# Four graph layers on one core: node steps between layer 2 and layer 3 run per half of the nodes

## The reference

```python
h = relu(layernorm(x)); x = x + relu((adj @ h) @ W.T + b)            # layer 0
h = relu(layernorm(x)); h, q, k = three Lorentz linear maps           # layer 1
att = adj * sigmoid((2 + 2 * (qm @ k.T)) / att_scale + att_bias)
support = att @ h; x = x + support / sqrt(|inner(support)|)
h = relu(layernorm(x))                                                # layer 2
w = adj / deg; log_ij = logmap(h_i, h_j)                              # for every pair i, j
agg = einsum('ij,ijc->ic', w, log_ij); x = x + expmap(0, agg @ weight + bias)
h = relu(layernorm(x)); x = x + w_last100(adj) @ (h @ weight) + bias  # layer 3
```

## Time and profile before

| | before |
|---|---|
| median of 3 runs | 1219.32 us (1218.47 to 1220.24) |
| profiled execution: time, span | 1219.28 us, 1217.5 us |
| PE, DVE, ACT, POOL busy | 89%, 70%, 62%, 32% of the span |
| mean granted TensorE clock | 0.94 |

### The profile page before, as it was taken

One profiled execution on the slowest core, in us unless ns is written; L12 is line 12 of the kernel. 1 busy time (PEld: TensorE's weight loads), 2 busy tenths in 40 slices (PEclk: granted clock), 3 DMA queues, 4 the chain that ended last, 5 costly groups with the idle time before them and its releaser, 6 DMA issues.

```text
span 1217.5 us, 15886 instructions
## 1 busy us (share of the span) xinstructions
PE 1081.6 (89%) x5064; PEld 503.5 (41%) x5084; DVE 851.6 (70%) x916; ACT 760.8 (62%) x780; POOL 393.4 (32%) x279
## 2 busy tenths in 40 slices
PE   2799999997699999999159999999999999954997
PEld 0233333336523333333124554555545454443555
DVE  7799989976756666666836767667677777666553
ACT  2355555552556666665258778778787888635864
POOL 6434423420101111110163334333343434323533
PEclk9799999997789999999569999999999999966999
DMA  9799999960068888885304545535454545211652
GB/s 325 263 351 358 350 341 339 359 250 9 1 196 287 280 281 286 288 281 180 128 0 140 171 133 179 173 124 187 139 173 138 181 131 157 67 54 44 205 184 86
DMA packets 96286, 237.97 MB, mean 195 GB/s; under 512 B 16369, under 2 KB 45041, under 8 KB 79857
## 3 DMA queue, kind: packets, MB, share of 16 engines
q1 hardware_dynamic: 87024, 220.62, 54.7%
q10 hardware_dynamic: 9216, 16.78, 3.6%
HBM read 219.55 MB, written 17.83 MB: 195 GB/s over the span
## 4 chain that ended last, share of the span: by engine, by line
PE 82%; DVE 8%; POOL 3%; issue 3%; ACT 2%; DMA 1%; SPq 0%; DVEq 0%; POOLq 0%; ACTq 0%
PE PS L452 55%; PE PS L649 10%; PE PS L595 5%; PE PS L596 4%; PE PS L672 4%; PE PS L484 1%; PE PS L462 1%; PE PS L474 1%; DVE st L1024 1%; DVE work L1021 1%; PE PS L696 1%; POOL work L408 1%; ACT work L766 1%; POOL X L401 1%; POOL brow L375 1%
## 5 line engine op out<-in xcount | busy, mean ns | idle before, releaser
L1161 DVE TENSOR_TENSOR work<-work,ring 128x1024 f32<-128x1024 f32 x128 | 151.2, 1222 | 88.6 <-ACT work L858 88.6
L415 POOL TENSOR_TENSOR ring<-work,ring 128x1024 f32<-128x1024 f32 x58 | 137.2, 2365 | 214.5 <-DVE work L1248 214.5
L801 ACT ACTIVATE work<-PS 128x1024 uint8<-128x1024 f32 x128 | 124.1, 1021 | 130.4 <-PE PS L452 130.4
L858 ACT ACTIVATE work<-PS,att_sc 128x1024 f32<-128x1024 f32 x128 | 147.4, 1201 | 88.7 <-PE PS L596 45.3
L452 PE MATMUL PS<-work,ystage 128*64 128x512 f32 x768 | 186.3, 606 | 0.1
L452 PE MATMUL PS<-ring,work 128*65 128x256 f32 (+1 forms) x568 | 183.2, 469 | 2.6 <-DVE work L1275 2.6
L1242 DVE SCALAR_TENSOR_TENSOR work<-PS,work 128x1024 f32<-128x1024 f32 x72 | 88.2, 1225 | 120.8 <-PE PS L452 107.6
L649 PE MATMUL PS<-TB,TA 65*128 65x512 f32 x288 | 139.8, 609 | 4.7 <-DVE work L1242 2.9
L381 POOL COPY ystage<-H 128x64 f32 x60 | 83.2, 1387 | 137.2 <-PE PS L452 136.9
L452 PEld LDWEIGHTS PS<-ring,work 128*65 128x65 f32 x568 | 77.2, 138 | 84.7 <-issue 62.8
L897 ACT ACTIVATE work<-work 128x1024 f32<-128x1024 f32 x72 | 76.0, 1055 | 46.1 <-DVE work L1242 45.9
(11 more groups left out here) (203 smaller groups left out, 1637.8 us busy)
## 6 DMA issues: line engine op xcount, KB each, us to landing
ring<-in_adj_t SPq DMA_DIRECT2D x96, 1024.0 KB, 5.2
ring<-in_adj_t SPq DMA_DIRECT2D x100, 512.0 KB, 3.8
work<-in_adj_t SPq DMA_DIRECT2D x32, 1024.0 KB, 7.7
...
```

The source lines that it names most:

```text
L415: nc.gpsimd.tensor_tensor(near(n), sum_[:, n % ROTS, :], near(n), ALU.mult).then_inc(sem("near_ready"), 1)
L801: nc.scalar.activation(made[:, k, u * UNIT:(u + 1) * UNIT], PS[:, (4 + 2 * u) * BANK:(6 + 2 * u) * BANK], ACT.Relu).then_inc(sem("codes_ma ...
L858: nc.scalar.activation(att[:, u % 2, :], PS[:, b * BANK:(b + 2) * BANK], ACT.Sigmoid, bias=att_sc[:, 2:3], scale=att_sc[:, 1:2]).then_inc( ...
L1161: V.tensor_tensor(prob[:, u, :], att[:, u % 2, :], ring[:, s, (u % 2) * UNIT:(u % 2 + 1) * UNIT], ALU.mult)\
```

## The change

- **Start.** The layernorm of layer 0 runs for group 1 alone first; that of group 0 stands between the first masks and degrees. POOL has four `ystage` buffers (`STAGES`) and starts at the first group; each of the eight bias pieces stands behind one staged tile.
- **Layer 1** is written out without loops, first all 32 source tiles for the first half of the targets, then for the second (64 steps). Weights are read from `HL` directly; POOL stages nothing.
- **First half's node steps** stand behind single steps of the second half's gather (`first_half1(o)`, o = 0 to 31).
- **Second half's node steps** stand behind units 0 to 13 (`second_half2(n)`); its rows are flipped behind units 12 and 13 (`FLIP1`).
- **Units** are in another order: 20 within the first half, 32 mixed (all mirrored), 20 within the second half; 12 segments where there were 8 strips.
- The `sums`, `Zn`, `GA` and `kap` buffers lie at other places, and loads for the first units start as ring slots come free.

```diff
-UNITS = [(S, p) for S in range(NS) for p in range(2 * S, T // 2)]
+UNITS = ([(S, p) for S in range(NS // 2) for p in range(2 * S, T // 4)]
+         + [(S, p) for S in range(NS // 2) for p in range(T // 4, T // 2)]
+         + [(S, p) for S in range(NS // 2, NS) for p in range(2 * S, T // 2)])
 NU = len(UNITS)
+N0 = sum(p < T // 4 for S, p in UNITS)
+FLIP1 = 12
...
+            for s in range(TG):
+                if s >= STAGES:
+                    pool.wait_ge(sem("agg0_done"), s - STAGES + 1)
+                nc.gpsimd.tensor_copy(ystage[:, s % STAGES, 0:D], H[:, T - 1 - s, :]).then_inc(sem("staged0"), 1)
+                if s >= STAGES:
+                    bias_piece(s - STAGES)
+            pool.wait_ge(sem("feats0_ready"), G)
...
+            def first_half1(o):
+                if o == 3:
+                    pe.wait_ge(sem("sums_out1"), 1)
+                    to_nodes(ident[:, :], 0, 0).then_inc(sem("support_ready"), 1)
+                if o == 18:
+                    pe.wait_ge(sem("support_used"), 1)
+                    pe.wait_ge(sem("zn_ready"), 1)
+                    flip_rows(PS[0:ROWS, 0:UNIT], 0, TG // 2).then_inc(sem("z_flipped"), 1)
+                if o == 22:
+                    pe.wait_ge(sem("zr_out"), 1)
+                    pe.wait_ge(sem("zl_out"), 1)
+                    pe.wait_ge(sem("kap_l_ready"), 1)
+                    flip_rows(PS[0:ROWS, 0:UNIT], TG // 2, TG).then_inc(sem("z_flipped"), 1)
+            for s in range(2 * T):
+                scores(s, 0)
+                scores(s, 1)
+                if s:
+                    gather1(s - 1, 0)
+                    gather1(s - 1, 1)
+                if s >= T:
+                    first_half1(s - T)
...
+            def second_half2(r):
+                pe.wait_ge(sem("zn_ready"), 2)
+                pe.wait_ge(sem("far_ready"), mirrors(FLIP1 + r - 1))
+                flip_rows(PS[0:ROWS, 4 * BANK:6 * BANK], TG + r * TG // 2, TG + (r + 1) * TG // 2).then_inc(sem("z_flipped"), 1)
...
+            def root_of(name, wait, before, g):
+                nc.scalar.preload_act_table_set("natural_log_exp_and_others")
+                power_of(name, st[2], st[1], -0.5, wait, before, (g,))
...
+            def first_half1(o):
+                if o == 1:
+                    one("sums_out1", TA[:, 0:UNIT], PS[:, 0:UNIT], ACT.Copy, ("agg1_done", 2 * T))
+                if o == 4:
+                    one("sup_sq", grp(sqr, 0), banks(0, 2).rearrange("p (t c) -> p t c", t=TG), ACT.Square, ("support_ready", 1))
+                if o == 6:
+                    root_of("sup_root", "sup_inner", 0, 0)
+                if o == 11:
+                    one("ln_sq", grp(sqr, 0), grp(cen, 0), ACT.Square, ("ln_centred", 2 * G + 1))
+                if o == 12:
+                    root_of("ln_sd", "ln_var", 2 * G, 0)
+                if o == 14:
+                    one("y_sq", grp(sqr, 0), grp(Y, 0)[:, :, 0:D], ACT.Square, ("feats2_ready", 1))
+                if o in (19, 23):
+                    r = (o - 19) // 4
+                    rows_out(slice(r * UNIT, (r + 1) * UNIT), PS[0:ROWS, 0:UNIT], ("z_flipped", r + 1))
+                if o in (20, 24):
...
+            def second_half2(n):
+                if n == 0:
+                    one("sup_sq", grp(sqr, 1), banks(4, 6).rearrange("p (t c) -> p t c", t=TG), ACT.Square, ("support_ready", 2))
+                if n == 2:
+                    power_of("sup_root", st[2], st[1], -0.5, "sup_inner", 1, (1,))
+                if n == 7:
+                    one("ln_sq", grp(sqr, 1), grp(cen, 1), ACT.Square, ("ln_centred", 2 * G + 2))
+                if n == 8:
+                    power_of("ln_sd", st[2], st[1], -0.5, "ln_var", 2 * G + 1, (1,))
+                if n == 9:
+                    one("y_sq", grp(sqr, 1), grp(Y, 1)[:, :, 0:D], ACT.Square, ("feats2_ready", 2))
+            def rows_out2(r):
+                for b in range(2):
+                    if b == 1:
+                        act.wait_ge(sem("zl_out"), 2 + 2 * r + 1)
+                    rows_out(slice(HALF + r * UNIT + b * BANK, HALF + r * UNIT + (b + 1) * BANK), PS[0:ROWS, (4 + b) * BANK:(5 + b) * BANK],
+                             ("z_flipped", 2 + r + 1))
...
+            sums_first(1)
+            means_first(1)
+            centre_first(1)
+            sums_first(0)
+            means_first(0)
+            spread_first(1)
+            feats_first(1)
...
+            mask0(1, 1, 16, True)
+            centre_first(0)
+            mask0(2, 2, 16, True)
+            degree0(0, 0, 0)
+            spread_first(0)
+            mask0(3, 3, 16, True)
+            degree0(0, 1, 1)
+            feats_first(0)
+            for k in range(4, RING0):
+                mask0(k, k, 16, False)
+                degree0(0, k - 2, k - 2)
+            for k in range(RING0 - 2, RING0):
+                degree0(0, k, k)
             for h in range(2):
...
+            def support_norm(g):
                 dve.wait_ge(sem("sup_sq"), g + 1)
                 chained(g, V.reduce_sum(grp(st[0], g), grp(sqr, g)[:, :, 1:D], AX.X))
-            for g in range(G):
                 hold(g)
                 chained(g, V.tensor_tensor(grp(st[1], g), grp(st[0], g), grp(sqr, g)[:, :, 0], ALU.subtract))
-            for g in range(G):
                 hold(g)
                 chained(g, V.scalar_tensor_tensor(grp(st[2], g), grp(st[1], g), -1.0, grp(st[1], g), ALU.mult, ALU.max))
...
+            def support_point(g, z):
+                rsqrt("sup_root", st[1], st[2], g, (g,))
+                hold(g)
+                V.tensor_tensor(grp(cen, g), z, over_c(st[2], g), ALU.mult).then_inc(sem("support_used"), 1)
+            def mean2(g):
+                chained(g, V.reduce_sum(grp(st[0], g), grp(X, g), AX.X))
+                hold(g)
+                chained(g, V.tensor_scalar(grp(st[0], g), grp(st[0], g), -1.0 / D, None, ALU.mult))
+            def centre2(g):
+                hold(g)
+                V.tensor_tensor(grp(cen, g), grp(X, g), over_c(st[0], g), ALU.add).then_inc(sem("ln_centred"), 1)
+            def spread2(g):
+                dve.wait_ge(sem("ln_sq"), 2 * G + g + 1)
+                chained(g, V.reduce_sum(grp(st[1], g), grp(sqr, g), AX.X))
+                hold(g)
+                V.tensor_scalar(grp(st[1], g), grp(st[1], g), 1.0 / D, EPS, ALU.mult, ALU.add).then_inc(sem("ln_var"), 1)
+            def feats2(g):
+                rsqrt("ln_sd", st[1], st[2], 2 * G + g, (g,))
+                norm_out(g, "feats2_ready", Y)
...
+            def first_half1(o):
+                z = banks(0, 2).rearrange("p (t c) -> p t c", t=TG)
+                if o == 4:
+                    support_norm(0)
+                if o == 7:
+                    support_point(0, z)
+                if o == 8:
+                    dve.wait_ge(sem("support_used"), 1)
+                    chained(0, V.tensor_tensor(grp(X, 0), grp(X, 0), grp(cen, 0), ALU.add))
+                if o == 9:
+                    hold(0)
+                    mean2(0)
+                if o == 10:
+                    centre2(0)
+                if o == 11:
+                    spread2(0)
+                if o == 13:
+                    feats2(0)
+                if o == 14:
+                    ball2(0)
+                if o == 15:
+                    signs2(0)
+                if o == 16:
+                    rows2(0)
+                if o in (19, 23):
+                    r = (o - 19) // 4
+                    scaled_rows(slice(r * UNIT, (r + 1) * UNIT), PS[0:ROWS, 0:UNIT], ("zr_out", r + 1))
+                if o in (20, 24):
+                    r = (o - 20) // 4
+                    V.tensor_copy(kap_l[0:ROWS, r * UNIT:(r + 1) * UNIT], PS[0:ROWS, 0:UNIT]).then_inc(sem("kap_l_ready"), 1)
...
+            def second_half2(n):
+                if n == 0:
+                    copy_out("support_out1", grp(cen, 1), banks(4, 6).rearrange("p (t c) -> p t c", t=TG), ("sup_sq", 2))
+                if n == 1:
...
+                    ball2(1)
+                if n == 10:
+                    signs2(1)
+                if n == 11:
+                    rows2(1)
+                if n in (FLIP1, FLIP1 + 1):
+                    r = n - FLIP1
+                    dve.wait_ge(sem("z_flipped"), 2 + r + 1)
+                    for b in (1, 0):
+                        if b == 0:
+                            dve.wait_ge(sem("zr_out"), 2 + 2 * r + 1)
+                        scaled_rows(slice(HALF + r * UNIT + b * BANK, HALF + r * UNIT + (b + 1) * BANK),
+                                    PS[0:ROWS, (4 + b) * BANK:(5 + b) * BANK], ("z_flipped", 2 + r + 1))
```

393 lines of the change are left out of this document (207 added, 186 removed).

## The result

The changed kernel takes 1185.93 us (median of 4 executions, 1183.4 to 1186.2) against 1218.89 us before (1217.65 to 1220.24): ratio 0.972, 95% interval 0.9702 to 0.9738. Its profiled execution took 1186.2 us, with a span of 1184.5. The forecast was 1176.0 us in a range of 1165 to 1189. The time lies in the range, 1.9 us above my own case's range and 10 us above the predicted value; where these 10 us are is the subject of what follows.

The account below looks back on a forecast made before the run. PE, busy 89% of the span, bounds the kernel, so gains lie only where it idles or runs slowly. 1219.3 - 11.5 - 46.0 + 3.9 + 3 + 7 = 1175.7, said as 1176 us, range 1165 to 1189.

Parts of the forecast that it names:

- my own case: The prediction's main case for the whole kernel: 1176 us, own range 1169 to 1184, chance 0.64.
- The start: Layer 0's opening: PE starts earlier with one group's features first, then DVE sets the pace; gain 11.5 us.
- Rival A: Layer 0's opening gives nothing, as POOL's bias pieces hold DVE their full 16.3 us; 1187 to 1188, chance 0.11.
- The gap: Last gather of layer 1 to unit 6: node steps hide under gather and units; gain 46.0 us.
- G: The last gather of layer 1, from which the first unit's sum was predicted 6.1 us later.
- my list: Units 0 to 5: intervals 6.1, 6.1, 5.0, 6.4, 5.3, 5.9 from PE, ACT and DVE work at full clock; 34.7 us.
- The gather: Layer 1's gather takes on first-half node steps: +3.9 us of PE work and +3 us of stalls.
- The units: Flips, second-half node steps and fast intervals lost among the units cost +7 us (3 to 11).
- the lock: Skill's rule: a GpSimd instruction holds a port shared with DVE exclusively; at the start only 0.67 us per degree was counted.
- the pattern: Unit intervals of the earlier kernel's profile, mirrored units at 6.47 us; 58.88 us from unit 6 to 16.
- B: Gather and units: delays pass along waiting lists, so covers fail, +20 against +10; 1186 to 1198, chance 0.14.
- D: Layer 1 written out: PE waits for instructions at each of 64 steps, slower than before; 1227 at 0.8 us, chance 0.02.

Follow-up runs that it names:

- the run with unread matmuls: Changed kernel plus three matmuls that nothing reads (65 rows x 512) behind the sides of each of units 0, 1 and 2; 1181.6 us.

## Why the prediction came out as it did

- **The start** held: 10.6 of 11.5. Tile 8's counts started at 53.12 (51 to 54 predicted) behind DVE's mask. That the figure came out so well is partly luck. The terms gave 51.2, and I took 53 in reserve; group 1's features then came 2 us late, for a reason not in the sum, since POOL's memset held a DVE step for 2.78 us, while the bias pieces cost 2.2 instead of 3. "DVE sets the pace" was the order of its list: with degrees put off, PE waits no more at these tiles, and the gain is 14.9. Rival A fell.
- **The gap** held in its shape: first sum at G + 6.0 (6.1 predicted). From there to unit 6 it took 37.9 instead of 34.7. "At full clock" was wrong (0.82), but the run with unread matmuls shows that this cost nothing. Three held steps stand in these units (1.33 at 588.59, 2.37 at 599.59, 1.32 at 614.09), 4.5 us beyond their 0.17, and the longest shows: unit 4's sum is 8.17 us behind unit 3's, where my list has 6.4. (The six intervals of my list add up to 34.8, not 34.7.) Moving them gave 0.9 of the 3.2 back, for the lump ahead of the min-multiply costs PE's mirrors a wait (1.48 us there), and POOL's residual add still holds DVE for 3.38; what would give the rest back, no run shows.
- **The gather** cost 5.0, not 6.9: each root with its two table loads delayed PE by 0.56, the low end of my 0.5 to 0.75, and all other steps stayed at 3.70, so DVE's lumps cost nothing of the 1.5 that I had set down.
- **The units** cost 10.4, not 7. Here a step of the reasoning failed. I had rejected the lock with the sentence "the rows show 0.67 us on a 2.33 us degree, and the sum goes by them", taken from the start, and did not ask what a lock would do in the units, where each node step stands right behind the operation that releases POOL's product. There four small steps of units 7 to 10 take 1.3 to 2.35 us. With them moved, units 6 to 16 cost 6.1 us over the pattern, near the 7 of my lists, whose parts were not measured one by one. The held steps account for the other 4.2 us, of which 2.2 are the low clock behind the wait for them and go away in executions where it returns sooner. Units 9 to 12 took 6.9 to 7.6 us each where I had named 5.5 to 6.5, and the granted clock of 1.00 throughout was wrong here too (0.64 from unit 10 to 12).
- **Behind the units** I had no term, and this is the largest miss, 5.0 us. The edit left that code as it was; DVE or POOL comes first there, by 0.0 to 0.4 us in most executions. POOL first costs 0.5 us up to layer 3 and 3.3 in it (66.3 against 65.8, 102.0 against 98.7). The other 1.2 us of the 5.0 stay with DVE first (65.83 + 98.7 against 65.48 + 97.8 before), and no run takes them apart. With DVE first the changed kernel takes 1182.2 us, 6.5 above my sum of 1175.7; the other terms (0.9 + 3.1 - 1.9 + 3.4 = 5.5) and this 1.2 make 6.7.
- **The range** held the time because it was wide. Four of the five terms missed to the same side, and only the gather's went the other way.
- **The rivals.** B (covers do not hold, 1186 to 1198) is nearest in time, at the low end that its own +20 against +10 gives, but not in cause: under the gather the covers held. D did not occur: layer 1's steps stayed at 3.70 us. Whether the kernel before ever falls into the slow course of layer 3 is open: only one of its executions was profiled, with DVE first by 0.33 us, and all 41 lie within 3.0 us.
